# Router dispatch of a mixture-of-experts block: last tiles that end at the last row, and paddings at fixed addresses

## The reference

```
h = layernorm(x) * (1 + cb) + sb
logits = silu(h @ rw1 + rb1) @ rw2 + rb2            # 8 experts
k_logits, k_index = top_k(logits, 2);  k_prob = softmax(k_logits)
for e in range(8):
    we = sum(where(k_index == e, k_prob, 0))
    out += we * (silu(h @ w1[e] + b1[e]) @ w2[e] + b2[e])
x = x + gb * out
```

## Time and profile before

| what | value |
|---|---|
| time, median of 3 runs | 314.01 us (312.12 to 314.21) |
| span of the profiled execution | 344.7 us |
| PE busy | 273.9 us, 79% |
| DVE busy | 196.8 us, 57% |
| ACT busy | 172.6 us, 50% |
| POOL busy | 164.5 us, 48% |
| PE's share of the chain that ended last | 58% |
| DVE's share of it | 14% |
| share of it under "another core or an unknown queue" | 8.7% |
| mean granted TensorE clock | 0.880 |

### The profile page before, as it was taken

How to read it: one execution, slowest core, us unless ns; L and a number is a source line. 1 busy time by engine, 2 the same in 40 slices (tenths; PEclk the granted TensorE clock), 3 DMA queues, 4 the chain that set the end, 5 groups by cost and what they waited for, 6 DMA issues and landing times.

```text
span 344.7 us, 5139 instructions
## 1 busy us (share of the span) xinstructions
PE 273.9 (79%) x1290; PEld 208.6 (61%) x1290; DVE 196.8 (57%) x730; ACT 172.6 (50%) x327; POOL 164.5 (48%) x181
## 2 busy tenths in 40 slices
PE   0877598996978856999934799999999999999400
PEld 0543246664546444868823578888888888888300
DVE  4989899876967643544450234444434444447626
ACT  1079988796867403532400444555555554555100
POOL 4322013378668471547575344544555445555700
PEclk9999698788797876986996699999999999999955
DMA  8990000011111151101122353222222365002366
GB/s 232 321 276 0 0 2 2 8 57 39 40 46 42 54 142 29 33 32 54 42 77 77 92 136 96 70 60 55 62 72 76 84 172 156 19 23 67 92 186 179
DMA packets 41080, 28.43 MB, mean 82 GB/s; under 512 B 4895, under 2 KB 37713, under 8 KB 41056
## 3 DMA queue, kind: packets, MB, share of 16 engines
q1 hardware_dynamic: 34034, 18.60, 20.1%
q0 software_dynamic: 4544, 8.47, 7.5%
q10 hardware_dynamic: 2478, 1.09, 1.2%
HBM read 16.39 MB, written 12.67 MB: 84 GB/s over the span
## 4 chain that ended last, share of the span: by engine, by line
PE 58%; DVE 14%; another core or an unknown queue 9%; ACT 8%; issue 5%; DMA 3%; POOL 1%; DVEq 1%; SPq 0%; POOLq 0%; ACTq 0%
PE bank L1052 20%; PE bank L1065 16%; PE bank L1001 7%; PE bank L1015 4%; PE bank L1041 3%; PE bank L1073 2%; PE bank L977 2%; PE bank L930 2%; PE bank L978 2%; DVE st L630 2%; DMA av<-expert_out 1%; ACT hT L525 1%; ACT hT L585 1%; DVE rows L725 1%
## 5 line engine op out<-in xcount | busy, mean ns | idle before, releaser
L492 POOL DMA_INDIRECT expert_out<-shared,tx x78 | 78.0, 1000 | 73.1 <-DVE shared L890 59.7
L585 ACT ACTIVATE hT<-bank,w_t 128x256 f32<-128x256 f32 x156 | 65.2, 471 | 45.5 <-PE bank L1052 26.1
L483 POOL DMA_INDIRECT sorted_rows<-rows,sloti x64 | 65.3, 1021 | 41.4 <-DVE sloti L769 23.8
L1052 PE MATMUL bank<-xT,w_t 128*128 128x256 f32 x312 | 79.8, 402 | 0.0
L1065 PE MATMUL bank<-hT,w_t 128*128 128x256 f32 x312 | 75.8, 387 | 0.1
L1052 PEld LDWEIGHTS bank<-xT,w_t 128*128 128x128 f32 x312 | 60.8, 204 | 8.9 <-issue 1.2
L1065 PEld LDWEIGHTS bank<-hT,w_t 128*128 128x128 f32 x312 | 57.8, 196 | 6.8 <-DVE w_t L882 0.3
L1001 PE MATMUL bank<-h2T,rw_s 128*128 128x512 f32 x64 | 41.5, 752 | 7.8 <-issue 3.9
L594 ACT ACTIVATE yT<-bank,w_t 128x256 f32<-128x256 f32 x39 | 18.5, 474 | 49.9 <-PE bank L1065 32.0
L864 DVE COPY xT<-bank 128x256 f32<-128x256 f32 x39 | 16.5, 424 | 39.3 <-PE bank L1041 21.8
L873 DVE COPY w_t<-w_s 128x516 f32 x39 | 17.2, 440 | 25.0 <-issue 13.9
(11 more groups left out here) (176 smaller groups left out, 354.6 us busy)
## 6 DMA issues: line engine op xcount, KB each, us to landing
tx<-sorted_rows SPq DMA_DIRECT2D x39, 130.0 KB
w_s<-in_L_ffn_w_dram SPq DMA_DIRECT2D x16, 256.0 KB, 6.2
xs<-in_L_attn_x_dram SPq DMA_DIRECT2D x8, 256.0 KB, 5.2
av<-expert_out SPq DMA_DIRECT2D x8, 256.0 KB, 3.8
qv<-expert_out SPq DMA_DIRECT2D x8, 256.0 KB, 5.4
expert_out<-shared,tx POOLq DMA_INDIRECT x78
sorted_rows<-padr SPq DMA_DIRECT2D x9, 130.0 KB
sorted_rows<-rows,sloti POOLq DMA_INDIRECT x64
```

What stands on the lines that cost most here:

```text
L483: p.indirect_dma_start(sorted_rows[:, :], bass.IndirectOffsetOnAxis(ap=sloti[:, k, t:t + 1], axis=0), rows[:, t, k, :], None).then_inc(s_d ...
L492: p.indirect_dma_start(expert_out[:, :], bass.IndirectOffsetOnAxis(ap=xr_i[:, s % U, n, D + 1:D + 2], axis=0), yo[:, s % U, n, :], None, b ...
L585: ins = nc.scalar.activation(hsT[:, u % 2, h, :], bank[4 + q][:, (h % 2) * SL:(h % 2 + 1) * SL], ACT.Silu, bias=w1_t[:, u % 2, HID + h:HID ...
L1052: ins = t.matmul(bank[4 + h // 2][:, (h % 2) * SL:(h % 2 + 1) * SL], w1_t[:, u % 2, h * P:(h + 1) * P], xT[:, u % 2, :], start=True, stop= ...
```

## The change

Each expert's region gets a head of 256 rows, and its rows begin behind it at `e * REG + 256`. The head is padding and its address is fixed, so all nine paddings are issued at the start of the kernel. An expert's last late tile starts 256 rows before the end of its rows, if it would otherwise reach over that end. It then holds rows that the tile before holds too. For these rows DVE computes a number past the end of `expert_out`, so that they are not written twice. `lim` is the last allowed start of a tile, `past` is by how many rows a tile was moved back; one matmul (`spread:0`) brings the 30 values of `past` to all partitions, one DVE operation (`drop:0`) compares them with the row numbers, and each `sc` of a late tile is preceded by an operation that writes the scatter's index into `target`. `pad_i` and its semaphore go.

```diff
+        lim = sb("lim", [1, NENT + 1])
+        past = sb("past", [1, LATE])
+        row_n = sb("row_n", [P, HALVES])
+        drop = sb("drop", [P, TILES, HALVES])
+        target = sb("target", [P, U, HALVES], I32)
-        cmpu = sb("cmpu", [1, 2, LATE, NENT])
+        cmpu = sb("cmpu", [1, 3, LATE, NENT])
...
-                l2:5 tx:8 l1:7 ty:5 l2:6 l1:8 ty:6 l2:7 tx:9 tx:10 l1:9 ty:7 l2:8 tx:11 l1:10 ty:8 l2:9 tx:12 l1:11
+                l2:5 tx:8 l1:7 ty:5 l2:6 l1:8 ty:6 l2:7 tx:9 spread:0 tx:10 l1:9 ty:7 l2:8 tx:11 l1:10 ty:8 l2:9 tx:12 l1:11
...
-                xT:11 w1:11 w2:9 sc:8 w1:12 w2:10 w2:11 xT:12 sc:9""",
+                xT:11 w1:11 w2:9 sc:8 w1:12 w2:10 w2:11 xT:12 drop:0 sc:9""",
...
             sp.wait_ge(s_const, 7)
-            padding(slice(NE * REG, NE * REG + SL))
+            for e in range(NE + 1):
+                padding(slice(e * REG, e * REG + SL))
...
-            sp.wait_ge(s_pads, 1)
-            for e in range(NE):
-                padding(bass.ds(sp.value_load(pad_i[0:1, e:e + 1], min_val=e * REG, max_val=e * REG + TOK), SL))
             sp.wait_ge(s_tab, 2)
             sp.wait_ge(s_pad, 16 * (NE + 1))
             sp.wait_ge(s_disp[1], 16 * TOPK * GPB * GT)
...
+                p.iota(iota_i[:, 32:32 + HALVES], pattern=[[P, HALVES]], base=0, channel_multiplier=1)
...
+                    index = xr_i[:, s % U, n, D + 1:D + 2] if s < EARLY else target[:, s % U, n:n + 1]
...
+                v.tensor_copy(row_n[:, :], iota_i[:, 32:32 + HALVES])
-                v.memset(taus2[:, 1, :], 0.0)
+                v.memset(lim[:, NENT:NENT + 1], float(NE * REG))
...
             def late_table(_):
                 dve.wait_ge(s_cnt, 2)
-                v.tensor_copy(pad_i[:, :], counted()[0:1, :]).then_inc(s_pads, 1)
+                v.tensor_scalar(lim[:, 0:NENT].rearrange("p (k e) -> p k e", k=2),
+                                counted()[0:1, :].unsqueeze(1).to_broadcast([1, 2, NE]), -float(SL), None, ALU.add)
...
+                v.tensor_tensor(val2[:, 2, :], lim[:, 1:NENT + 1], lim[:, 0:NENT], ALU.subtract)
...
-                link(v.tensor_tensor(cmpu[:, :, :, :], cmpt[:, :, :].unsqueeze(1).to_broadcast([1, 2, LATE, NENT]),
-                                     val2[:, :, :].unsqueeze(2).to_broadcast([1, 2, LATE, NENT]), ALU.mult))
+                link(v.tensor_tensor(cmpu[:, :, :, :], cmpt[:, :, :].unsqueeze(1).to_broadcast([1, 3, LATE, NENT]),
+                                     val2[:, :, :].unsqueeze(2).to_broadcast([1, 3, LATE, NENT]), ALU.mult))
                 link(v.tensor_reduce(tf[:, :, :], cmpu[:, :, :, :], AX.X, ALU.add))
-                link(v.tensor_tensor(tf[:, :, :], tf[:, :, :], taus2[:, :, :], ALU.add))
-                v.tensor_scalar(tab[:, :, EARLY:TILES], tf[:, :, :], float(NE * REG), None, ALU.min).then_inc(s_tab, 1)
+                link(v.tensor_tensor(tf[:, 0, :], tf[:, 0, :], taus2[:, :], ALU.add))
+                v.scalar_tensor_tensor(past[:, :], tf[:, 0, :], lim[:, 0:1], tf[:, 2, :], ALU.subtract,
+                                       ALU.subtract).then_inc(s_past, 1)
+                v.tensor_copy(tab[:, 1, EARLY:TILES], tf[:, 1, :])
+                v.scalar_tensor_tensor(tab[:, 0, EARLY:TILES], tf[:, 2, :], lim[:, 0:1], tf[:, 0, :], ALU.add,
+                                       ALU.min).then_inc(s_tab, 1)
                 dve.wait_ge(s_tab, 2)
+
+            def dropped(_):
+                dve.wait_ge(s_spread, 1)
+                link(v.tensor_tensor(drop[:, EARLY:TILES, :], spread().unsqueeze(2).to_broadcast([P, LATE, HALVES]),
+                                     row_n[:, :].unsqueeze(1).to_broadcast([P, LATE, HALVES]), ALU.is_gt))
...
+                if not (static(s) and s < EARLY):
+                    v.scalar_tensor_tensor(target[:, u, :], drop[:, bass.ds(s, 1), :].rearrange("p a n -> p (a n)"),
+                                           float(TOPK * TOK), xr_i[:, u, :, D + 1], ALU.mult, ALU.add)
                 v.tensor_tensor(yo[:, u, :, :], bank[1][:, 0:SL].rearrange("p (n d) -> p n d", n=HALVES),
                                 xr[:, u, :, D:D + 1].to_broadcast([P, HALVES, D]), ALU.mult).then_inc(s_yo, 1)
...
+            def spread_past(_):
+                pe.wait_ge(s_past, 1)
+                t.matmul(spread(), ones_row[:, :], past[:, :], start=True, stop=True).then_inc(s_spread, 1)
```

More of the change, by code:

```diff
@@ L154, in adaln_block @@
         val1 = sb("val1", [1, 2, NE])
-        val2 = sb("val2", [1, 2, NENT])
+        val2 = sb("val2", [1, 3, NENT])
         taken = sb("taken", [1, NE])
@@ L160, in adaln_block @@
         cmpt = sb("cmpt", [1, LATE, NENT])
-        cmpu = sb("cmpu", [1, 2, LATE, NENT])
-        tf = sb("tf", [1, 2, LATE])
+        cmpu = sb("cmpu", [1, 3, LATE, NENT])
+        tf = sb("tf", [1, 3, LATE])
         tab = sb("tab", [1, 2, TILES], I32)
-        pad_i = sb("pad_i", [1, NE], I32)
         xr = tx[:, 0:U * HALVES * ROW].rearrange("p (u n r) -> p u n r", u=U, n=HALVES)
@@ L199, in adaln_block @@
             "s_mask", "s_pos")
[L200 to L201 removed]
+        s_dlt, s_tdl, s_slot, s_cnt, s_tab, s_pad, s_past, s_spread = sems(
+            "s_dlt", "s_tdl", "s_slot", "s_cnt", "s_tab", "s_pad", "s_past", "s_spread")
         s_disp = sems("s_disp0", "s_disp1")
@@ L220, in counted, with spread @@
             return bank[6][:, 2 * GT * NE:2 * GT * NE + NE]
+        def spread():
+            return bank[6][:, 3 * P:3 * P + LATE]
         def gate_bank(g):
@@ L804, in constants @@
                 v.memset(val2[:, 1, NENT - 1:NENT], 0.0)
-                v.tensor_scalar(mboth[:, 0, 0, :], eid[:, 0, :], float(REG // P), None, ALU.mult)
-                link(v.tensor_scalar(ereg[:, :], eid[0:1, 0, :], float(REG), None, ALU.mult))
+                v.tensor_scalar(mboth[:, 0, 0, :], eid[:, 0, :], float(REG // P), float(SL // P), ALU.mult, ALU.add)
+                link(v.tensor_scalar(ereg[:, :], eid[0:1, 0, :], float(REG), float(SL), ALU.mult, ALU.add))
             def residual_stats(g):
@@ L820, in early_table @@
                                      upto[:, 0:NE].unsqueeze(1).to_broadcast([1, EARLY, NE]), ALU.is_ge))
-                link(v.tensor_tensor(cmpu[:, :, 0:EARLY, 0:NE],
+                link(v.tensor_tensor(cmpu[:, 0:2, 0:EARLY, 0:NE],
                                      cmpt[:, 0:EARLY, 0:NE].unsqueeze(1).to_broadcast([1, 2, EARLY, NE]),
                                      val1[:, :, :].unsqueeze(2).to_broadcast([1, 2, EARLY, NE]), ALU.mult))
-                link(v.tensor_reduce(tf[:, :, 0:EARLY], cmpu[:, :, 0:EARLY, 0:NE], AX.X, ALU.add))
-                v.tensor_tensor(tab[:, :, 0:EARLY], tf[:, :, 0:EARLY], taus[:, :, 0:EARLY], ALU.add).then_inc(s_tab, 1)
+                link(v.tensor_reduce(tf[:, 0:2, 0:EARLY], cmpu[:, 0:2, 0:EARLY, 0:NE], AX.X, ALU.add))
+                v.tensor_tensor(tab[:, :, 0:EARLY], tf[:, 0:2, 0:EARLY], taus[:, :, 0:EARLY], ALU.add).then_inc(s_tab, 1)
                 dve.wait_ge(s_tab, 1)
@@ L834, in entries @@
                 link(v.scalar_tensor_tensor(base[:, NE:NENT], full[:, :, 0], float(SL), ereg[:, :], ALU.mult, ALU.add))
-                v.tensor_scalar(taus2[:, 0, :], taus[:, 0, :], base[:, 0:1], None, ALU.add)
+                v.tensor_scalar(taus2[:, :], taus[:, 0, :], base[:, 0:1], -float(SL), ALU.add, ALU.add)
                 link(v.tensor_tensor(dbase[:, :], base[:, 1:NENT + 1], base[:, 0:NENT], ALU.subtract))
@@ L896, in _ @@
                            "resid": residual_stats, "norm2": ln2_norm, "top2": top2, "place": place,
-                           "table1": early_table, "table1b": entries, "table2": late_table,
+                           "table1": early_table, "table1b": entries, "table2": late_table, "drop": dropped,
                            "xT": lambda s: take_x(s, s % U), "w1": lambda s: weights1(s, s % U),
@@ L1077, in _ @@
                            "turn_x": xn_transpose, "gates": gate_products, "turn_y": y_transpose,
-                           "turn_h": h2_transpose, "router": router, "logits": logits, "rank": ranks, "count": count,
+                           "turn_h": h2_transpose, "router": router, "logits": logits, "rank": ranks, "count": count, "spread": spread_past,
                            "tx": lambda s: turn_rows(s, s % U), "l1": lambda s: layer1(s, s % U),
```

8 lines of the change are left out of this document (4 added, 4 removed).

## The result

| | before | changed |
|---|---|---|
| median, 12 runs each, in turn | 313.85 us (311.65 to 315.91) | 317.38 us (314.88 to 319.15) |
| ratio changed / before | | 1.0113, 95% interval 1.0085 to 1.0140 |

What follows compares the result with a forecast made beforehand. PE was taken as the bound, its idle time ahead of the fully busy loop counting one for one. Terms 0 + 1.25 + 0.2 + 0.1 = +1.55 us on 314.0 gave 315.6 us, range 312.4 to 319.0 us.

Steps and rivals of the forecast that it cites:

- The unknown pieces as a cost of profiling: Four chain pieces under no known cause, together 29.3 us, come from profiling and are absent from timed runs.
- sums in differences: Over the whole kernel, the change's terms are summed as differences and added to the unprofiled 314.0 us.
- Eight paddings, 0: Between the second table's counts and tile 9's load: hidden, load 0.6 us ahead of PE, so removal gains 0.
- The rival that PE waited for them: At `tx:9`, PE waited about 2.5 to 3 us for tile 9; removing paddings gains 1.4 us: 312.6 us; chance 18%.
- The longer table, +1.25 us: DVE's second table, on PE's path ahead of `ty:4`, gets longer: +1.25 us, with 1.0 and 1.6 as ends.
- The rival of a hidden table: PE comes late to `ty:4`, so the second table's +1.25 us vanishes: 314.3 us; chance 10%.
- Targets, drop, spread: `target` operations in the loop, `drop` ahead of `sc:9` and `spread:0` ahead of `tx:10` are hidden: 0 each.
- The 0.2 us at the end: At the kernel's serial end, two `target` operations ahead of `sc` aren't hidden: +0.2 us (0.1 to 0.5).
- the 0.1 us of `row_n`: The copy for `row_n` in DVE's constants, where DVE is itself on the chain: +0.1 us.
- The clock: PE's longer idle time ahead of `ty:4` draws a half-clock stretch of 6.83 us, up to 3.4 us: 319.0 us; chance 17%.
- the gap before may have paid this already: PE's old idle time ahead of `ty:4`, 1.5 to 2.8 us, may already draw the half clock; argument against The clock.

Runs made afterwards that it cites:

- the undisturbed profile: The kernel before, unchanged, timed and profiled once more: 313.82 us, ratio 1.0001; its profiled execution took 315.68 us.
- the short table: Small tiles of both tables laid over 30 partitions: in the kernel before, paddings kept, 314.25 us, ratio 1.0024; in the changed kernel 312.54 us, ratio 0.9941.
- the filling: Unused PE matmuls ahead of `ty:4`: seven in the changed kernel, 315.29 us; four in the kernel before, 314.01 us; six in that with an unused third table column, 315.68 us.
- the third column alone: The kernel before with an unused third column in the second table's product and reduction, paddings kept: median 318.13 us; ratio 0.9998, taken without the upper eight executions.
- the upper group: No edit: the slower twelve of the changed kernel's 24 executions, 317.32 to 319.23 us, mean 318.5; the other twelve have mean 315.4.

## Why the prediction was wrong

The forecast was +1.55 us, 315.6; measured was +3.5 us by the medians and +2.9 by the means of all runs. The direction and the range held; the sum was too small by half, and a loss of over 1% had only 16%. By its steps:

- **The unknown pieces as a cost of profiling, and sums in differences.** Right: the undisturbed profile has a span of 313.8 us and none of them.
- **Eight paddings, 0.** Right, with its working: load of tile 9 issued at T + 12.0 for T + 12.1, landed at T + 14.2 for T + 14.1, wanted at T + 14.8 for T + 14.7. Four more paddings made PE wait at once, so the margin was as thin as it said. The rival that PE waited for them is out; with the short table it would have been true (1.88 us). It was also priced too high: at 1.5 us each, seven more steps of 0.37 us are 2.6 us, and less the margin a wait of 2.0 us, not 3.
- **The longer table, +1.25 us, "every us of table is a us more".** Right in kind, a little small: 6.08 - 4.63 = 1.45 us in the trace. Timed behind the filling, what remains is 1.0 us (0.2 to 1.9) in the changed kernel and 1.4 us (0.6 to 2.2) with the third column alone. The two large instructions were sized right (1.66 us each in the sum, 1.65 and 1.64 measured); the small ones took 0.2 us more together than I gave them. The rival of a hidden table is out: in all profiles the later table end reaches `tx:9` in full.
- **Targets, drop, spread.** Nothing in the loop, PE at 99.9%. `tx:9` to `tx:10` takes 1.00 us with `spread:0` between them and 0.99 to 1.00 without. The 0.2 us at the end wasn't resolved; nor was the 0.1 us of `row_n`.
- **The clock, left out of the sum and kept as a rival with 17%.** This is the step that failed. I had the right mechanism and the right gap (2.7 to 4.1 us forecast, 3.2 to 3.3 measured), and let "the gap before may have paid this already" talk me out of it. Filling the gap before gives nothing (-0.2 us, -1.1 to 0.8), so it had paid nothing that could be measured; filling the new gap takes 2 us off. The price of one stretch was put too high (up to 3.4 us; the row lasts 6.83 us, this one 3.4 us, with idle time in part of it, and costs 1.3 to 1.4), and I took it as one answer for all executions, while the runs show it in some only.

The Trainium skill (TensorE: Matmul & The Clock Gate, section "Why this matters for your kernels") warns of long idle time between bursts of matmuls. By the filling the long gap costs clock in the mean, as the page says; in the single case the runs don't follow it: of four idle times of 3.2 to 3.3 us two were followed by the lower level, and so was one of 2.55 us (four more paddings).

What stays open: 1.4 us of table and 1.3 us of clock in half the executions make 2.1 us, where the means say 2.9 (2.1 to 3.6). Where the rest lies, if it is real, no run here says. The clocks on record don't bear out that executions at low clock are commoner with the long gap. In the kernel before 95 executions have their mean granted clock on record, and 42 of them lie at 0.902 or lower, where the upper group would lie without its 3.4 us at half clock behind the table (worth 0.005); that is 44%, against 12 of 24. What differs is the price: those 42 take 314.7 us and the other 53 take 313.7, while the two groups of the changed kernel are 3.1 us apart. With the gap filled 5 of 12 executions still have 0.898 or less, and take 315.1 to 316.8 us. That an upper-group time means a stretch behind the table is seen in both upper profiles and inferred for the other ten. What decides whether the gap draws the lower level is open too. The kernel without the mask of the shared rows wasn't tried: two scatters under way at once would write the same rows.

## What to carry to other kernels

A wait of the engine that sets the end costs its length, and it can cost the clock as well: when a change lengthens a gap of TensorE, price the gap with and without a half-clock stretch behind it, and give the second a real share of the chance. Before you remove a queue of transfers, work out when the tile it holds up is wanted; here the transfers were 0.6 us from mattering, and what made their removal pay was a shorter chain on another engine. A control with useless work in the gap tells length from clock in one experiment.

## What the hardware showed

- One DVE operation over 1440 elements took 1.65 us on one partition and 0.20 us as 48 elements on each of 30 partitions, so this small table was better off across partitions even at the price of two matmuls and a copy to turn them back.
- The same idle time of 3.2 us drew the 1.2 GHz level in two of four profiled executions, and in both the clock had been at half for 6.8 us until some 14 us before, which isn't shown to be the cause; an idle time of 2.55 us (four more paddings) drew it once, one of 2.92 us (third column) didn't in the one profile of it, and one of 1.84 us didn't.
- A padding DMA whose address SP reads from a table took 8.45 us for eight, a fixed one 5.72 us for nine at the kernel's start and 2.10 us for four behind the others: 1.06 us each against 0.64 and 0.53, so a padding with an address read from a table cost SP up to twice a fixed one. How much of the difference is the reading itself isn't separated.
